# GpSimd adds the two halves of each head's exponentials before VectorE sums them

## The chip, the core and the metric

One core of a Trainium2 chip runs the whole program. TensorE (PE in the rows, its weight loads PEld), VectorE (DVE), ScalarE (ACT), GpSimd (POOL) and SyncE (SP, which here only starts transfers) each work through an instruction list of their own, in order, and meet at semaphores. The metric is the device time of one execution in microseconds (us).

## The reference

A perceiver block on x of 4 x 256 tokens with 256 features: cross attention to 4096 context rows, then local attention, then a mixture of experts. Each stage is added to x. What matters here is the local attention: 16 heads of 16 features, windows of 64 queries that see 128 keys (their own window and the one before), cut by a mask, and a softmax over the keys.

```
scores = jnp.einsum('bnqhd,bnkhd->bnhqk', Qb, Kw) / math.sqrt(dh)
scores = jnp.where(mask[None, :, None, :, :], scores, -jnp.inf)
wts = jax.nn.softmax(scores, axis=-1)
out = jnp.einsum('bnhqk,bnkhd->bnqhd', wts, Vw).reshape(B, N, D)
return out @ o_w.T + o_b
```

## The kernel before, in words

The program has three parts in time. Until about 258 us: cross attention, bound by TensorE. From there to about 338 us: local attention. Then the routing of tokens to experts, and from about 358 us to the end 23 tiles of expert products, in which TensorE works without a pause and the expert weights stream in.

Local attention is cut into 16 units (`WORK`): for each of 4 batch entries, 2 tiles of 128 tokens (t) times 2 halves of the heads (8 heads each, `HPC`). One unit holds 128 queries x 8 heads x 128 keys, so 128 x 1024 numbers; it lies in `local[u]`, of which there are four, part of `region_a`. Unit n goes through these steps:

- TensorE: `local_score(n)`, masks and scores into four PSUM banks (lines 1355, 1360, 1365). There is only one set of these banks, so the scores of unit n wait until VectorE has read those of unit n-1 (`less_max`).
- VectorE: `local_max(n)`, the maximum per head (L963) and the subtraction into `local[u]` (L968, signals `less_max`).
- ScalarE: `local_softmax(n)`, the exponential in place (L788, signals `local_exp`).
- VectorE: `local_sum(n)`, the sum of 128 columns per head (L974) and its reciprocal (L976, signals `inv_ready`).
- GpSimd: the product with the reciprocal, in place (L594, signals `normed`).
- TensorE: `local_turn(n)`, eight transposes (L1290) into two PSUM banks; ScalarE copies them out (`local_evict`, L677); TensorE `local_weigh(n)` multiplies with the values (L1502); ScalarE copies the result out (`local_out`, L801).

The order on each engine is written out by hand. TensorE runs turn(n), score(n+3), weigh(n-1), and then, beside ten of the units, one projection of queries, keys or values of a later batch entry (`FILL_AT`, L1346). VectorE runs sum(n+1), max(n+3). ScalarE runs the copies of unit n, the output of n-1, the exponential of n+3, the projection's copy. GpSimd has only the products, and between them three small jobs: four small operations after unit 2 (`root_second`, L529 to L539), one after unit 3 (L599), and the addition of a bias row to 128 x 512 numbers after unit 5 (`rows_biased`, L546).

`silu0` and `silu1` are parts of `region_w`; they are written only in the expert stage, and nothing lives there during local attention.

Of the kernel before, what the change touches and what calls it, by code (L numbers as in the profile page):

```python
# [8 lines left out]
ALU = mybir.AluOpType  # L9
ACT = mybir.ActivationFunctionType  # L10
X_AXIS = mybir.AxisListType.X

P = 128
# [8 lines left out]
BANK = 512  # L22
# [5 lines left out]
HEADS, DH, WIN = 16, 16, 64  # L28
HPC = P // DH
# [7 lines left out]
WORK = [(b, u) for b in range(BATCH) for u in range(len(UNITS))]  # L37
# [45 lines left out]
def perceiver(nc, x, ctx, ctx_cols, first_weights, w2_b, second_weights, third_weights, o_b, up_weights, down_weights, out):  # L83
    stack = ExitStack()
    with stack:
        def sb(name, cols, dt=F32):
            return stack.enter_context(nc.sbuf_tensor(name, [P, cols], dt))

        def sem(name):
            return stack.enter_context(nc.semaphore(name))  # L90
# [10 lines left out]
        def cut(region, widths):  # L101
            at, parts = 0, []
            for w in widths:
                parts.append(region[:, at:at + w])
                at += w
            assert at <= region.shape[1], (at, region.shape)
            return parts
# [9 lines left out]
        k_side = k_side_f.rearrange("p (a c n) -> p a c n", a=SIDES, c=DC)  # L117
        local = [s.rearrange("p (h k) -> p h k", h=HPC) for s in (sl0, sl1, sl2, sl3)]
        _, pT_f, _, headsT_f = cut(region_s, [TILES * D, 4 * BANK, DC * TOK, DC * TOK])
        pT = pT_f.rearrange("p (r k n) -> p r k n", r=4, k=TPG)  # L120
        v_wide = v_wide_f.rearrange("p (t h n) -> p t h n", t=BATCH * STRIPS, h=HEADS)
# [3 lines left out]
        w_up = [region_a[:, at * MAT:(at + 2) * MAT] for at in (0, 2, 6)]  # L125
        w_down = [region_a[:, (4 + n) * MAT:(5 + n) * MAT] for n in range(2)]
        x3n_f, place_row_f, place_prob_f, _, xrT_f, place_tile_f, _ = cut(
            region_s, [TILES * D, PICKS * P // 2, PARTS * PICKS * EVEN // 2, PICKS * P // 2 - PARTS * PICKS * EVEN // 2,
                       DC * TOK, PARTS * PICKS * EVEN // 2, DC * TOK - PARTS * PICKS * EVEN // 2])
# [2 lines left out]
        xrT = xrT_f.rearrange("p (c n) -> p c n", c=DC)  # L132
        hid = [xrT_f[:, n * INNER:(n + 1) * INNER] for n in range(2)]
        *xg, hidT0, hidT1, yt0, yt1, silu0, silu1 = cut(region_w, [D] * AHEAD + [INNER] * 2 + [D] * 2 + [INNER] * 2)
        hidT, yt, silu = [hidT0, hidT1], [yt0, yt1], [silu0, silu1]
        _, last_tokens, same = cut(region_w, [RAW * DC * BANK - 2 * P, P, P])
        before_last = sb("tokens_before_last", 1)

# [7 lines left out]
        def two_parts(name, cols):  # L146
# [50 lines left out]
        hmax, hsum, hinv = [sb(name, len(UNITS) * HPC)[:, :].rearrange("p (u h) -> p u h", u=len(UNITS))  # L197
                            for name in ("head_max", "head_sum", "head_inv")]
# [58 lines left out]
        zeroed = sem("zeroed")  # L257
        masks_ready, sides_ready = sem("masks_ready"), sem("sides_ready")
        local_done, row_max, less_max, local_exp = sem("local_done"), sem("row_max"), sem("less_max"), sem("local_exp")
        row_sum, inv_ready, normed = sem("row_sum"), sem("inv_ready"), sem("normed")  # L260
        local_turned, localT_ready, localpv_done = sem("local_turned"), sem("localT_ready"), sem("localpv_done")
        heads_ready = sem("heads_ready")
# [75 lines left out]
        def over_keys(cols):  # L338
            return cols.rearrange("p (h a) -> p h a", a=1).broadcast_to([P, HPC, P])
# [117 lines left out]
        def _(pool):  # L457
# [76 lines left out]
            def root_second(b):  # L534
                two = slice(2 * b, 2 * b + 2)
                root(b, SECOND_AT[b], ROOT_SECOND[b])
                nc.gpsimd.tensor_tensor(shift[:, two], mv[:, two, 0], rstd[:, two], ALU.mult).then_inc(shifting, 1)
                pool.wait_ge(shifting, b + 1)
                nc.gpsimd.tensor_tensor(shift[:, two], zeros[:, 0:2], shift[:, two], ALU.subtract).then_inc(bias2_ready, 1)  # L539

            def rows_biased(b):
                part = xr[:, b * TPB:(b + 1) * TPB, :]
                if b == 0:
                    pool.wait_ge(ob_loaded, 16)
                pool.wait_ge(xn_ready, SECOND_AT[b] * TPB)
                nc.gpsimd.tensor_tensor(part, part, obr[:, :].rearrange("p (a d) -> p a d", a=1).broadcast_to([P, TPB, D]),  # L546
                                        ALU.add).then_inc(biased, 1)
# [9 lines left out]
            for b in range(BATCH):  # L557
                n = b % 2
# [30 lines left out]
            nc.gpsimd.memset(v_wide_f[:, KEPT:], 0.0).then_inc(zeroed, 1)  # L589


            for n, (b, u) in enumerate(WORK):
                pool.wait_ge(inv_ready, n + 1)
                nc.gpsimd.tensor_tensor(local[u], local[u], over_keys(hinv[:, u, :]), ALU.mult).then_inc(normed, 1)  # L594
                if n == LAST_ROOT:
                    root_second(BATCH - 1)
                if n == GATE_CENTRED:
                    pool.wait_ge(heads_ready, GATE_MEAN + 1)
                    nc.gpsimd.tensor_tensor(gate, gwT, gate_mean[:, :].rearrange("p (a e) -> p a e", a=1).broadcast_to([P, DC, E]),  # L599
                                            ALU.subtract).then_inc(gate_centred, 1)  # L600
                if n == LAST_BIAS:
                    rows_biased(BATCH - 1)
# [294 lines left out]
        def _(dve):  # L897
# [72 lines left out]

            def local_sum(n):
                b, u = WORK[n]
                dve.wait_ge(local_exp, n + 1)
                nc.vector.tensor_reduce(hsum[:, u, :], local[u], axis=X_AXIS, op=ALU.add).then_inc(row_sum, 1)  # L974
                dve.wait_ge(row_sum, n + 1)
                nc.vector.reciprocal(hinv[:, u, :], hsum[:, u, :]).then_inc(inv_ready, 1)  # L976

# [128 lines left out]

            local_max(1)
            local_sum(0)
            local_max(2)
            for n in range(len(WORK)):  # L1110
                if n + 1 < len(WORK):
                    local_sum(n + 1)
                if n + LOOK < len(WORK):
                    local_max(n + LOOK)
                if n == 0:
                    statistics(range(TILES - TPB, TILES))
# [115 lines left out]
            def tile_y(j, n):  # L1232
# [7 lines left out]
                else:  # L1240
# [7 lines left out]
                                    axis=X_AXIS, op=ALU.add).then_inc(tokens_ready, 1)  # L1248
            for j in range(SLOT_TILES):
                n = j % 2  # L1250
# [485 lines left out]
```

## Time and profile before

| | |
|---|---|
| median of 3 runs | 600.28 us (600.08 to 600.31) |
| the profiled execution's own time | 599.96 us |
| its span, first to last instruction | 598.2 us |
| granted TensorE clock, mean | 0.989 |
| PE busy | 571.6 us, 96% |
| DVE busy | 414.6 us, 69% |
| ACT busy | 332.5 us, 56% |
| POOL busy | 254.5 us, 43% |

Busy is time in which an engine has an instruction in work; for TensorE the ends are modelled, so a busy PE need not be at its peak. The share is a mean over stages that have different limits. In the rows, "[1.04 <-POOL region_a L594]" means that the engine stood idle for 1.04 us before this instruction and that the signal which ended the idle time came from GpSimd's line 594. PEclk 1.00 is the full clock of 2.4 GHz, 0.50 is 1.2 GHz.

### The profile page before, as it was taken

Reading aid. Unit: us, or ns where it says so; the run is one execution under the profiler, and the core shown is the slowest. Engines: PE = TensorE matmul, PEld = TensorE weight load, DVE = VectorE, ACT = ScalarE, POOL = GpSimd, SP = SyncE. Lnnn points to the kernel's source line nnn. Section 1 sums busy time; section 2 is a strip of 40 time slices with the busy share of each in tenths; the row PEclk is TensorE's granted clock in tenths of the full one; section 3 lists DMA queues with packets and bytes.
Section 4 is the critical chain, followed back from the end, with each engine's and each line's share of the span. In section 5 each row is a group of like instructions: output and inputs, shape, how many; then the busy total and the mean of one; then the engine's idle time right before and its main releaser. Section 6 shows DMA issues by size and latency. Waiting matters only on the chain.

```text
span 598.2 us, 9977 instructions
## 1 busy us (share of the span) xinstructions
PE 571.6 (96%) x3765; PEld 487.6 (82%) x3765; DVE 414.6 (69%) x701; ACT 332.5 (56%) x564; POOL 254.5 (43%) x259
## 2 busy tenths in 40 slices
PE   7799999999999999989999989999999999999995
PEld 5589988998799889967676867888888888888884
DVE  3866686668656865579888688676767676777761
ACT  4337535753476455628766827565647474747450
POOL 6366347534742484334544620333333333333212
PEclk9999999999999999999999989999999999999998
DMA  8993086008600200000002966999999999999642
GB/s 291 424 413 157 1 329 233 1 2 324 239 1 2 71 1 2 1 1 1 2 2 75 397 260 240 339 323 342 332 345 329 339 333 354 337 343 323 226 154 88
DMA packets 25166, 119.27 MB, mean 199 GB/s; under 512 B 2640, under 2 KB 8912, under 8 KB 14096
## 3 DMA queue, kind: packets, MB, share of 16 engines
q1 hardware_dynamic: 20752, 112.48, 49.9%
q0 software_dynamic: 4368, 6.16, 5.3%
q8 instruction: 30, 0.49, 0.3%
q14 instruction: 16, 0.13, 0.1%
HBM read 113.52 MB, written 6.42 MB: 200 GB/s over the span
## 4 chain that ended last, share of the span: by engine, by line
PE 80%; DVE 11%; ACT 2%; issue 2%; POOL 2%; DMA 2%; POOLq 0%; SPq 0%; DVEq 0%; ACTq 0%
PE psum L1653 20%; PE psum L1430 14%; PE psum L1670 13%; PE psum L1384 12%; PE psum L1290 11%; PE psum L1346 2%; DVE head_max L963 2%; DVE region_a L968 1%; DMA region_w<-ctx_cols_dram 1%; PE psum L1528 1%; POOL wide_low L562 1%; DVE wide_low L985 1%; PE psum L1312 1%; PE psum L1392 1%; PE psum L1502 1%
## 5 line engine op out<-in xcount | busy, mean ns | idle before, releaser
L677 ACT ACTIVATE wide_high<-region_a 128x1024 fp32r<-128x1024 f32 (+1 forms) x104 | 105.2, 1011 | 97.7 <-PE psum L1653 90.2
L1120 DVE TENSOR_TENSOR wide_low<-region_a,wide_high 128x1024 fp32r<-128x1024 f32 x92 | 112.4, 1224 | 58.2 <-ACT wide_high L677 58.2
L1670 PE MATMUL psum<-region_a,region_w 128*128 128x256 f32 x368 | 83.3, 379 | 0.0
L1430 PE MATMUL psum<-turned_high,wide_low 128*128 128x256 f32 x256 | 78.6, 307 | 2.9 <-DVE turned_low L1046 2.4
L1046 DVE TENSOR_TENSOR turned_low<-psum,turned_high 128x512 fp32r<-128x512 f32 x64 | 43.7, 690 | 54.2 <-ACT turned_high L677 54.1
L1653 PE MATMUL psum<-wide_low,turned_high 128*128 128x512 f32 x184 | 78.2, 425 | 0.2 <-DVE turned_high L1222 0.2
L1670 PEld LDWEIGHTS psum<-region_a,region_w 128*128 128x128 f32 x368 | 69.7, 190 | 10.0
L1653 PE MATMUL psum<-wide_high,turned_low 128*128 128x512 f32 x184 | 72.5, 394 | 0.0
L1430 PE MATMUL psum<-turned_high,wide_high 128*128 128x256 f32 x256 | 72.2, 282 | 0.0
L1430 PE MATMUL psum<-turned_low,wide_high 128*128 128x256 f32 x256 | 72.1, 282 | 0.0
L1653 PE MATMUL psum<-wide_high,turned_high 128*128 128x512 f32 x184 | 72.1, 392 | 0.0
L1290 PE MATMUL psum<-ident,region_s 128*128 128x128 f32 x448 | 63.0, 273 | 0.9 <-DVE region_s L923 0.4
L629 POOL TENSOR_TENSOR pool_pause<-zeros 128x1 f32<-128x1 f32 x21 | 4.0, 191 | 139.1 <-DVE region_w L1239 139.1
L677 ACT ACTIVATE turned_high<-psum 128x512 fp32r<-128x512 f32 x64 | 37.9, 599 | 40.8 <-PE psum L1430 40.2
L562 POOL TENSOR_TENSOR wide_low<-region_w,wide_high 128x1024 fp32r<-128x1024 f32 x12 | 31.9, 2657 | 66.2 <-ACT wide_high L677 66.2
L1030 DVE TENSOR_SCALAR_CACHE_REDUCE region_s<-psum 128x512 f32<-128x512 f32 x64 | 43.2, 687 | 22.1 <-PE psum L1384 22.1
L722 ACT ACTIVATE region_s<-region_s,neg_max 128x512 f32<-128x512 f32 x64 | 45.9, 718 | 19.9 <-DVE neg_max L1034 19.9
L1384 PE MATMUL psum<-wide_high,wide_low 128*128 128x512 f32 x128 | 51.7, 404 | 5.4 <-DVE wide_low L985 4.3
L1290 PEld LDWEIGHTS psum<-ident,region_s 128*128 128x128 f32 x448 | 51.6, 140 | 6.0 <-ACT region_s L722 2.0
L576 POOL CAST wide_high<-region_a 128x512 fp32r<-128x512 f32 x52 | 36.5, 710 | 44.7 <-PE psum L1430 35.5
L677 ACT ACTIVATE wide_high<-region_w 128x1024 fp32r<-128x1024 f32 x32 | 33.6, 1059 | 38.7 <-PE psum L1384 28.9
L1430 PEld LDWEIGHTS psum<-turned_high,wide_low 128*128 128x128 f32 x256 | 48.5, 189 | 4.3 <-POOL wide_low L579 2.5
(223 smaller groups left out, 1196.3 us busy)
## 6 DMA issues: line engine op xcount, KB each, us to landing
region_a<-up_weights_dram SPq DMA_DIRECT2D x23, 2048.0 KB, 9.1
region_a<-down_weights_dram SPq DMA_DIRECT2D x23, 1024.0 KB, 7.3
region_w<-ctx_cols_dram SPq DMA_DIRECT2D x32, 512.0 KB, 9.3
region_a<-ctx_dram SPq DMA_DIRECT2D x16, 1024.0 KB, 12.2
third_weights<-third_weights_dram SPq DMA_DIRECT2D x1, 1035.0 KB, 26.0
residual<-x_dram SPq DMA_DIRECT2D x4, 256.0 KB, 7.8
sums_by_token<-residual SPq DMA_DIRECT2D x2, 512.0 KB, 9.5
normed_rows<-region_s SPq DMA_DIRECT2D x4, 256.0 KB, 6.6
```

The source lines that it names most:

```text
L562: nc.gpsimd.tensor_tensor(ctxT_lo[:, split_of(b, ch)], raw[(b * CHUNKS + ch) % RAW], ctxT_hi[:, split_of(b, ch)].bitcast(F32), ALU.subtrac ...
L576: nc.gpsimd.tensor_copy(val_hi[:, at], part).then_inc(val_high, 1)
L677: return nc.scalar.activation(dst, src, ACT.Copy)
L722: nc.scalar.activation(part, part, ACT.Exp, bias=nmax[:, t:t + 1], accum_out=lpart[:, t, k:k + 1]).then_inc(exp_done, 1)
L1030: nc.vector.tensor_scalar(scores[t][:, ch * BANK:(ch + 1) * BANK], score_bank(ch, t), float(D) ** -0.5, LOWEST, ALU.mult, ALU.max, accum_o ...
L1046: nc.vector.tensor_tensor(pT_lo[:, g % 2], probs_bank(g).rearrange("p (k n) -> p k n", k=PAIR), pT_hi[:, g % 2].bitcast(F32), ALU.subtract ...
L1120: nc.vector.tensor_tensor(w_lo[:, k % RING], group_of(k), w_hi[:, k % RING].bitcast(F32), ALU.subtract).then_inc(low_ready, 1)
L1290: return nc.tensor.transpose(dst, src, ident[0:src.shape[0], 0:src.shape[0]])
L1384: last = nc.tensor.matmul(score_bank(ch, t), q[:, n, c, t * P:(t + 1) * P], k[:, split_of(b, ch), c, :], start=c == 0 and m == 0, stop=c = ...
L1430: last = nc.tensor.matmul(bank[6 + c][:, 0:NTOK], v[:, value_slot(b, g), k, c * P:(c + 1) * P], p[:, g % 2, k, :], start=g == 0 and k == 0 ...
L1653: last = nc.tensor.matmul(bank[g], rows[:, n, cols], w[:, (4 * j + g) % RING, c, :], start=c == 0 and m == 0, stop=c == DC - 1 and m == le ...
L1670: last = nc.tensor.matmul(to[:, 0:D], hidT[n][:, ic * P:(ic + 1) * P], rows, start=ic == 0, stop=ic == IC - 1)
```

## The change

Before the sum, GpSimd adds columns 64 to 127 of each head to columns 0 to 63, into one of two areas of 128 x 512 in `silu0`; VectorE then sums 64 columns per head in place of 128. The sum no longer waits for the exponential but for the new addition (`halved`), which waits for the exponential. The exponentials themselves stay as they are for the product. GpSimd's list becomes: add 0, add 1, product 0, add 2, product 1, add 3, and so on.

```diff
+        halves = [h.rearrange("p (h k) -> p h k", h=HPC) for h in (silu0[:, 0:BANK], silu0[:, BANK:])]
...
+            def add_halves(n):
+                u = WORK[n][1]
+                pool.wait_ge(local_exp, n + 1)
+                nc.gpsimd.tensor_tensor(halves[n % 2], local[u][:, :, 0:WIN], local[u][:, :, WIN:P], ALU.add).then_inc(halved, 1)
+
+            add_halves(0)
+            add_halves(1)
             for n, (b, u) in enumerate(WORK):
                 pool.wait_ge(inv_ready, n + 1)
                 nc.gpsimd.tensor_tensor(local[u], local[u], over_keys(hinv[:, u, :]), ALU.mult).then_inc(normed, 1)
+                if n + 2 < len(WORK):
+                    add_halves(n + 2)
                 if n == LAST_ROOT:
                     root_second(BATCH - 1)
...
             def local_sum(n):
                 b, u = WORK[n]
-                dve.wait_ge(local_exp, n + 1)
-                nc.vector.tensor_reduce(hsum[:, u, :], local[u], axis=X_AXIS, op=ALU.add).then_inc(row_sum, 1)
+                dve.wait_ge(halved, n + 1)
+                nc.vector.tensor_reduce(hsum[:, u, :], halves[n % 2], axis=X_AXIS, op=ALU.add).then_inc(row_sum, 1)
```

GpSimd's list at the start of local attention, before. L594 is the product; the four rows behind it are `root_second`.

```order
L594 TENSOR_TENSOR region_a<-region_a,head_inv 128x1024 [waits inv_ready] x3
L529 TENSOR_TENSOR ln_sd<-ln_mean_var,eps 128x2 [waits var_ready]
L531 TENSOR_TENSOR ln_rstd<-ln_sd,minus_half 128x2 [waits sd_ready]
L537 TENSOR_TENSOR ln_shift<-ln_mean_var,ln_rstd 128x2 [waits rstd_ready]
L539 TENSOR_TENSOR ln_shift<-zeros,ln_shift 128x2 [waits shifting]
```

The same place on GpSimd now. L597 is the new addition, L603 the product, L531 to L541 are `root_second`.

```order
L597 TENSOR_TENSOR region_w<-region_a 128x512 [waits local_exp] x2
L603 TENSOR_TENSOR region_a<-region_a,head_inv 128x1024 [waits inv_ready]
L597 TENSOR_TENSOR region_w<-region_a 128x512 [waits local_exp]
L603 TENSOR_TENSOR region_a<-region_a,head_inv 128x1024 [waits inv_ready]
L597 TENSOR_TENSOR region_w<-region_a 128x512 [waits local_exp]
L603 TENSOR_TENSOR region_a<-region_a,head_inv 128x1024 [waits inv_ready]
L597 TENSOR_TENSOR region_w<-region_a 128x512 [waits local_exp]
L531 TENSOR_TENSOR ln_sd<-ln_mean_var,eps 128x2 [waits var_ready]
L533 TENSOR_TENSOR ln_rstd<-ln_sd,minus_half 128x2 [waits sd_ready]
L539 TENSOR_TENSOR ln_shift<-ln_mean_var,ln_rstd 128x2 [waits rstd_ready]
L541 TENSOR_TENSOR ln_shift<-zeros,ln_shift 128x2 [waits shifting]
```

Every product but the last two now stands behind the addition of a later unit, which waits for that unit's exponential. The order on the other engines is the same.

## Rows read from the trace of the kernel before

**Rows 1.** Stretches: busy us and instructions of PE, PEld, DVE, ACT, POOL; PEclk, DMA, GB/s.
```profile
258.00:332.00 74.00, 68.65 (x801) 50.08 (x800) 65.45 (x80) 47.72 (x93) 36.61 (x23) 1.00 0.09 33
345.00:598.20 253.20, 244.34 (x1248) 205.79 (x1247) 174.72 (x255) 137.13 (x185) 79.15 (x70) 0.99 0.85 294
```
**Rows 2.** Waits, 260 to 332 us: us in total, times, longest.
```profile
POOL region_a L594 <- DVE head_inv L976: 36.2, 15, 5.1
...
DVE head_max L963 <- PE psum L1365: 4.0, 5, 1.3
...
PE psum L1290 <- POOL region_a L594: 1.6, 3, 1.0
```
**Rows 3.** Timeline, 321 to 327 us, units 11 to 15: start, duration, engine, line.
```profile
321.49 1.23 DVE L968 TENSOR_TENSOR region_a<-psum,head_max 128x1024 f32<-128x1024 f32 x1
...
322.40 1.04 PE L1290 MATMUL psum<-ident,region_a 128*128 128x128 f32 x8
322.63 1.21 DVE L974 TENSOR_REDUCE head_sum<-region_a 128x8 f32<-128x1024 f32 x1
322.75 1.06 ACT L788 ACTIVATE region_a<-region_a 128x1024 f32<-128x1024 f32 x1 [1.32 <-DVE region_a L968]
...
323.27 0.60 PE L1355 MATMUL psum<-mask_bf,ident_bf 128*128 128x256 bf16 x4
...
323.88 0.20 DVE L976 RECIPROCAL head_inv<-head_sum 128x8 f32<-128x8 f32 x1
324.16 1.90 POOL L594 TENSOR_TENSOR region_a<-region_a,head_inv 128x1024 f32<-128x1024 f32 x1 [2.05 <-DVE head_inv L976]
...
324.60 1.23 DVE L963 TENSOR_REDUCE head_max<-psum 128x8 f32<-128x1024 f32 x1 [0.52 <-PE psum L1365]
...
325.93 1.23 DVE L968 TENSOR_TENSOR region_a<-psum,head_max 128x1024 f32<-128x1024 f32 x1
...
326.11 1.09 PE L1290 MATMUL psum<-ident,region_a 128*128 128x128 f32 x8 [1.04 <-POOL region_a L594]
```
**Rows 4.** Durations by line: ns least, median, most; first and last start.
```profile
L594 POOL TENSOR_TENSOR region_a<-region_a,head_inv x16: 1895/1897/1898, 267.0 to 330.4; 128x1024 f32<-128x1024 f32 x16
...
L546 POOL TENSOR_TENSOR residual<-residual,ob_rows x4: 1280/1284/1288, 94.5 to 291.3; 128x512 f32<-128x512 f32 x4
...
L579 POOL TENSOR_TENSOR wide_low<-region_a,wide_high x32: 1272/1292/2262, 35.7 to 245.3; 128x512 fp32r<-128x512 f32 x32
```
**Rows 5.** VectorE's groups by form: busy us and mean ns of one.
```profile
L1090 DVE TENSOR_TENSOR residual<-residual,psum 128x512 f32<-128x512 f32 x3 | 2.0, 664 | 0.0
```
**Rows 6.** Timeline, the first units, all engines.
```profile
266.02 1.05 ACT L788 ACTIVATE region_a<-region_a 128x1024 f32<-128x1024 f32 x1
...
267.04 1.90 POOL L594 TENSOR_TENSOR region_a<-region_a,head_inv 128x1024 f32<-128x1024 f32 x1 [5.05 <-DVE head_inv L976]
...
268.99 1.10 PE L1290 MATMUL psum<-ident,region_a 128*128 128x128 f32 x8 [0.18 <-POOL region_a L594]
...
272.50 1.22 DVE L968 TENSOR_TENSOR region_a<-psum,head_max 128x1024 f32<-128x1024 f32 x1
```
**Rows 7.** Timeline of GpSimd: the two jobs between the products.
```profile
277.94 0.20 POOL L529 TENSOR_TENSOR ln_sd<-ln_mean_var,eps 128x2 f32<-128x2 f32 x1
...
279.27 0.20 POOL L539 TENSOR_TENSOR ln_shift<-zeros,ln_shift 128x2 f32<-128x2 f32 x1
...
291.34 1.28 POOL L546 TENSOR_TENSOR residual<-residual,ob_rows 128x512 f32<-128x512 f32 x1
```
**Rows 8.** Timeline of TensorE, one unit with a full projection.
```profile
295.95 1.04 PE L1290 MATMUL psum<-ident,region_a 128*128 128x128 f32 x8
...
298.57 1.99 PE L1346 MATMUL psum<-xnT,third_weights 128*128 128x256 f32 x8
300.40 1.04 PE L1290 MATMUL psum<-ident,region_a 128*128 128x128 f32 x8
```
**Rows 9.** Two short stretches, columns as in rows 1.
```profile
260.00:264.00 4.00, 3.00 (x20) 1.85 (x19) 3.93 (x7) 1.06 (x1) 1.98 (x1) 1.00 0.00 0
344.00:348.00 4.00, 3.70 (x24) 2.22 (x25) 2.96 (x14) 1.72 (x5) 0.20 (x1) 0.50 1.08 395
```

More of the change, by code:

```diff
@@ L259, in perceiver @@
         local_done, row_max, less_max, local_exp = sem("local_done"), sem("row_max"), sem("less_max"), sem("local_exp")
+        halved = sem("halved")
         row_sum, inv_ready, normed = sem("row_sum"), sem("inv_ready"), sem("normed")
```

## The prediction, made before the result was known

> **What bounds the kernel now.** I read the stretches first, since the change touches local attention alone. There TensorE is busy 68.65 of 74 us and VectorE 65.45; GpSimd has the most room, 36.61 of 74 [rows 1]. The waits say who is late. GpSimd waits 36.2 us in total for VectorE's reciprocal; VectorE waits for scores, 4.0 us for one form of them; TensorE waits only 1.6 us, three times, for GpSimd's product [rows 2]. So no single engine sets the pace. A unit with a full projection costs TensorE 300.40 - 295.95 = 4.45 us back to back [rows 8]; where there is less beside it, a loop through the engines decides.
>
> That loop is read in the timeline of units 11 to 15 [rows 3]. Call S(n) the start of the subtraction L968 of unit n. From S(14) at 321.49: the sum of unit 13 starts 1.14 us later (322.63), its reciprocal 1.25 later (323.88), the product 0.28 later (324.16), the transposes of unit 13 1.95 later (326.11, TensorE idle 1.04 before them). The steps behind are read one unit earlier: transposes 322.40, scores 323.27 (0.87), maximum 324.60 (1.33), subtraction 325.93 (1.33). The scores behind turn(13) are those of unit 16, which does not exist; for lower units they are those of n+3. So S(n+2) leads by sum(n+1), product(n+1), turn(n+1), score(n+4) to S(n+4): 1.14 + 1.25 + 0.28 + 1.95 + 0.87 + 1.33 + 1.33 = 8.15 us for two units. There are two such loops, one of even units and one of odd. TensorE's 4.45 per full unit (8.90 for two) is the longer of the two limits in most of the stage; over the stage the kernel takes S(15) - S(3) = 325.93 - 272.50 = 53.43 us for 12 units [rows 3, 6], 8.9 for two.
>
> **The change, part by part.**
>
> *VectorE's sum* goes from 1.21 us [rows 3] to 512 inputs. A 512 form takes 664 ns where the 1024 form of L968 takes 1225 [rows 3, 5], so 512 fewer cost 0.56 less: about 0.65, and 16 x 0.56 = 9 us less VectorE busy time. It is hidden or worse, as the next part shows.
>
> *GpSimd's addition* is new: 16 x 128x512 with two real operands. The nearest row is L546, an addition with the same count of outputs: 1284 ns, once in this very stage beside VectorE's sum [rows 4, 7]. I take 1.28, so 20.5 us more GpSimd busy time. The low end is half of the product's 1897, 0.95; the high end is the slowest L579, 2.26 [rows 4]. Below zero is excluded, it is added work.
>
> The Trainium skill ("GPSIMD Engine Reference", section "3.1 Elementwise — side-by-side cycle accounting") puts a two-input addition at some 2.6 cycles of 1.2 GHz per element. For 512 that would be an estimate of 1.11 us, which makes the sum below 4.6 in place of 5.6; the trace has 1.28 for this count, and that is used.
>
> *The new wait* is where the time goes. GpSimd works in order, and product(n+1) now stands behind add(n+2), which waits for the exponential of unit n+2. From S(n+2): the exponential starts 322.75 - 321.49 = 1.26 later and takes 1.06; with 0.07 to reach GpSimd and 1.23 from start to start for the addition (its 1.28 less the overlap seen between neighbours), product(n+1) can start 3.63 us after S(n+2). Before it started 1.14 + 1.25 + 0.28 = 2.67 after. The shorter sum does not help: sum(n+1) needs only add(n+1), done a unit earlier, and the reciprocal is ready about 1.14 + 0.70 + 0.28 = 2.12 after S(n+2), but the product is not next in the list. So the loop becomes 8.15 + 0.96, about 9.13 us for two units (4.56 per unit), above TensorE's 4.45. Queued behind the late product are turn(n+1), and on TensorE behind that score(n+4), weigh(n), and the projection; VectorE's max(n+4) waits for that score.
>
> *The sum over the stage*, on the odd loop, which reaches the last unit:
> - Start. Product 0 stands behind add 1, which waits for exp(1), done at 266.02 + 1.05 = 267.07. Add 1 ends at 268.40, product 0 starts there and not at 267.04: +1.35, about 1.3 of which turn(0), at 268.99, score(3) and S(3) take over [rows 6]. S(3) = 273.8.
> - Six rounds from S(3) to S(15): 6 x 9.13 = 54.8.
> - In one of them the bias job after unit 5 (1.28, 1.25 net) stands between add(7) and product 6; before it lay in idle time [rows 7]. +1.25. The four small operations after unit 2 (277.94 to 279.47, 1.5 us) now delay product 3 in the same way. That falls on the even loop; the two loops share TensorE, and a turn, a score or a projection of the one standing ahead of the other's costs 0.1 to 0.5 us at four places. I put all of this at 1.4.
> - S(15) = 273.8 + 54.8 + 1.25 + 1.4 = 331.25 against 325.93: +5.3.
> - Behind it TensorE runs without a pause, and its backlog (13 late product, output rows, two last units) adds 0.2 to 0.3. Local attention ends 5.6 later.
>
> Routing is a chain of dependent steps and the expert stage has TensorE busy 244.34 of 253.20 us [rows 1]; nothing there gives time back. The weights' first load starts when the last scores are done, so it moves with them. Profile: 599.96 + 5.6 = 605.6; on the median of the runs (0.32 above the profiled execution) 605.9.
>
> **The rivals.**
>
> *It is faster.* Place: the product after the reciprocal. If the additions fitted into GpSimd's 36.2 us of waiting [rows 2] and never stood ahead of a ready product, each of some five bound rounds would gain up to the sum's 0.56, 2.8 us in all: 597.5. It decides at the point where add(n+2) is over when the reciprocal n+1 arrives: 2.12 after S(n+2). The exponential alone ends 2.32 after, so even a free addition does not get there. Chance 3%.
>
> *No change.* TensorE, at 93% busy, would hide the late products: turn(6) is at 295.95 with no idle time before it [rows 8]. The slack before a turn is 1.5 us at most, and it is used up in the first units because 9.13 is above 8.90. 600.3. Chance 3%.
>
> *The addition is cheaper* (0.95). The loop becomes 8.80, the start +1.0; TensorE decides more often: +3.8, 604.1. Chance 14%.
>
> *The addition is stretched* by VectorE beside it, to the 2.26 seen once for L579. Seven times 0.98 more on the loop, and TensorE no cover any more, bring about 12 us: 612. Against it: the product kept 1895 to 1898 ns in all 16 cases beside VectorE's maxima, subtractions and sums [rows 4]. Chance 4%.
> The Trainium skill ("SBUF — State Buffer", section "Who interferes with whom") says that a VectorE instruction with two SBUF inputs and a GpSimd one that reads SBUF exclude each other. In this stage VectorE's large operations have one SBUF or PSUM tensor, so by that rule too the addition keeps its time, and the 16 rows agree.
>
> *The clock falls.* TensorE will idle some 6 us more. The clock stayed at 1.00 with 3.00 of 4 us busy, and was 0.50 at 344 to 348, behind the small products of the routing [rows 9]. A fall in the stage for 4 to 8 us would cost half of that on TensorE's work: 2 to 4 more, 608 to 610. A shift of the low spell in routing is worth up to 1 us either way. Chance 6%.
>
> **How the numbers follow.** The forecast holds 70%, with its own range 604.6 to 607.2 (addition 1.1 to 1.4, TensorE places 0.5 to 2.4). The range reaches to the cheap addition and to part of the clock case: 603.4 to 608.3. What a measurement of this kernel can tell from no change is 0.2%, 1.2 us. Slower: 70 + 14 + 4 + 6 = 94, less 1 for what I may have overlooked, 93%; same 3.5%; faster 3.5%.
>
> **What the profile after would show.** L597 16 times at about 1280 ns; the sum (L985) at about 650 ns. GpSimd busy near 275 us and VectorE near 406. Product 0 starts near 268.4, not 267.0; in late units it starts 3.6 us after the subtraction of the next unit, directly behind an addition, and GpSimd waits for ScalarE's exponential. TensorE waits for the product in more than three places, some 7 us in all. S(15) lies near 331.3, and from there all steps lie 5.3 to 5.8 later. I am wrong if the product starts within 2.7 us of that subtraction, if GpSimd's products are not behind additions, if the addition is far from 1.28, or if the delay of local attention is not the same as that of the end.

## The result and the profile after

| | before | after |
|---|---|---|
| median of 4 runs | 600.18 us (598.35 to 600.31) | 606.12 us (604.40 to 611.34) |
| ratio | | 1.0134, 95% interval 1.0106 to 1.0162 |
| profiled execution, its span | 599.96, 598.2 us | 604.40, 602.6 us |
| GpSimd busy | 254.5 us | 274.6 us |
| VectorE busy | 414.6 us | 405.9 us |

The kernel is slower. The forecast was 605.9 us in a range of 603.4 to 608.3. A second comparison, of 6 runs with 23 of before, gave 1.0081 (1.0053 to 1.0110), so the loss is between 3 and 10 us, 4.6 and 5.9 by the two medians. Both intervals lie clear of no change.

The waits from 260 to 337 us, where [rows 2] has those of before:

```profile
POOL region_w L597 <- ACT region_a L799: 24.8, 15, 3.1
...
DVE head_max L974 <- PE psum L1376: 11.4, 8, 2.8
...
DVE head_max L974 <- PE psum L1371: 8.3, 6, 3.4
PE psum L1301 <- POOL region_a L603: 7.0, 9, 1.5
```

L597 is the addition, L603 the product, L985 the sum. GpSimd no longer waits for the reciprocal at all. It waits for the exponential, 15 times, and what TensorE waits for the product grew from 1.6 us in 3 places to 7.0 in 9. VectorE's saved time came back as waiting for scores: 19.7 us now, 6.2 before (4.0 behind L1365 and 2.2 behind L1360, the lines that are L1376 and L1371 here). Durations by line (ns least, median, most):

```profile
L597 POOL TENSOR_TENSOR region_w<-region_a x16: 1266/1270/1275, 261.8 to 333.7; 128x512 f32<-128x512 f32 x16
...
L603 POOL TENSOR_TENSOR region_a<-region_a,head_inv x16: 1892/1897/1901, 267.4 to 336.8; 128x1024 f32<-128x1024 f32 x16
...
L985 DVE TENSOR_REDUCE head_sum<-region_w x16: 654/676/687, 264.6 to 335.0; 128x8 f32<-128x512 f32 x16
```

The loop, in the timeline from 326 to 332 us. These are units 12 to 15 as in [rows 3]:

```profile
326.40 1.23 DVE L979 TENSOR_TENSOR region_a<-psum,head_max 128x1024 f32<-128x1024 f32 x1
327.54 0.68 DVE L985 TENSOR_REDUCE head_sum<-region_w 128x8 f32<-128x512 f32 x1
327.66 1.06 ACT L799 ACTIVATE region_a<-region_a 128x1024 f32<-128x1024 f32 x1 [1.63 <-DVE region_a L979]
...
328.25 0.20 DVE L987 RECIPROCAL head_inv<-head_sum 128x8 f32<-128x8 f32 x1
...
328.79 1.27 POOL L597 TENSOR_TENSOR region_w<-region_a 128x512 f32<-128x512 f32 x1 [1.12 <-ACT region_a L799]
...
330.02 1.90 POOL L603 TENSOR_TENSOR region_a<-region_a,head_inv 128x1024 f32<-128x1024 f32 x1
...
331.31 1.23 DVE L979 TENSOR_TENSOR region_a<-psum,head_max 128x1024 f32<-128x1024 f32 x1
...
331.97 0.33 PE L1301 MATMUL psum<-ident,region_a 128*128 128x128 f32 x1 [1.52 <-POOL region_a L603]
```

The reciprocal of unit 13 is out at 328.45, and GpSimd is idle until 328.79. It does not start product 13, because addition 14 is next in its list and that waits for the exponential. The product starts at 330.02, 3.62 us after the subtraction at 326.40 (3.63 was forecast, 2.67 before). It shows no idle time of its own: an engine that is never idle before an instruction can still have made it late, by what it was told to do first.

A second thing is in this profile that is not in the one of before. Stretches from 293 us on, columns as in [rows 1]:

```profile
293.00:294.00 1.00, 0.20 (x1) 0.20 (x2) 0.99 (x2) 0.65 (x2) 0.74 (x1) 0.87 0.00 0
294.00:295.00 1.00, 1.00 (x6) 1.00 (x6) 0.20 (x1) 1.00 (x3) 0.44 (x1) 0.50 0.00 0
...
296.00:297.00 1.00, 1.00 (x7) 0.59 (x9) 0.00 (x0) 0.40 (x1) 1.00 (x1) 0.50 0.00 0
297.00:298.00 1.00, 1.00 (x24) 0.45 (x20) 0.38 (x1) 0.00 (x0) 1.00 (x2) 0.92 0.00 0
```

TensorE ran at 1.2 GHz for some 3.4 us, behind two waits that the timeline of TensorE shows:

```profile
291.99 0.63 PE L1301 MATMUL psum<-ident,cross_outT 128*128 128x128 f32 x4 [0.67 <-ACT cross_outT L710]
293.80 1.97 PE L1301 MATMUL psum<-ident,region_a 128*128 128x128 f32 x8 [1.18 <-POOL region_a L603]
```

The eight transposes took 1.97 us instead of 1.09.

From here on "stage length" is the distance from the subtraction of unit 0 to that of unit 15. It is read from one profile and leaves out what the clock does before and behind the stage. Before: 325.93 - 260.40 = 65.53. After: 331.31 - 259.45 = 71.86, so +6.33.

### The profile page after: what moved, and what is told of

Same layout as the page of the kernel before. It is cut to its first block, busy times and chain, and to the rows that moved or that the text cites. A ratio compares the mean times of both kernels' runs of the same rounds, so it can differ in the third digit from the quotient of the medians.

```text
span 602.6 us, 9993 instructions
## 1 busy us (share of the span) xinstructions
PE 574.7 (95%) x3765; PEld 488.9 (81%) x3765; DVE 405.9 (67%) x701; ACT 332.5 (55%) x564; POOL 274.6 (46%) x275
## 4 chain that ended last, share of the span: by engine, by line
PE 78%; DVE 9%; POOL 5%; issue 3%; DMA 2%; ACT 2%; POOLq 0%; DVEq 0%; ACTq 0%
PE psum L1664 19%; PE psum L1441 14%; PE psum L1395 12%; PE psum L1681 12%; PE psum L1301 11%; PE psum L1357 2%; POOL region_a L603 2%; DVE head_max L974 1%; POOL region_w L597 1%; DVE region_a L979 1%; PE psum L1323 1%; ACT region_a L799 1%; POOL wide_low L564 1%; PE psum L1539 1%; PE psum L1403 1%
```

## The experiments

| kernel | stage length | median us | ratio to before, 95% |
|---|---|---|---|
| before | 65.53 | 599.13 and 599.86 | 1 |
| changed, again (e1) | 71.84 | 603.72 | 1.0081 (1.0053 to 1.0110) |
| product first (e2) | 64.35 | 599.61 | 1.0013 (0.9996 to 1.0029) |
| additions, full sum (e3) | 71.85 | 602.61 | 1.0066 (1.0044 to 1.0088) |
| short sum, no additions (e4) | 64.73 | 598.77 | 0.9990 (0.9976 to 1.0004) |
| filled waits (e5) | 71.42 | 605.27 | 1.0087 (1.0056 to 1.0118) |
| bias job first (e6) | 70.28 | 603.81 | 1.0084 (1.0054 to 1.0114) |
| half additions (e7) | 68.29 | 602.30 | 1.0047 (1.0025 to 1.0068) |
| product first, plain tail (e8) | 64.36 | 598.37 | 0.9974 (0.9956 to 0.9993) |

e1 to e4 were measured beside one set of 23 runs of the kernel before (median 599.13), e5 to e8 beside a second of 29 (599.86).

**The changed kernel again (e1).** No edit.

> The changed kernel once more, unaltered, to see how much of its distance is the same in every execution. Stage length here and below means: start of unit 0's subtraction to start of unit 15's, 65.53 us before and 71.86 in the first profile of the changed kernel, of which I put 0.9 to 1.0 down to 3.4 us at half the TensorE clock inside the stage. Theory (product behind the addition in GpSimd's list): 70.9 without such a clock spell, 71.9 with it, end +5 to +6 us. Rival (the clock spell is the larger part of the loss and comes and goes): without it the end is within 3 us of the kernel before.

71.84, and half clock again, from about 294.7 to 298.1 us. Its six runs went from 602.19 to 606.94 us. The three with a mean clock of 0.990 to 0.993 took 602.2 to 602.6, the three at 0.984 to 0.987 took 604.8 to 606.9. The runs of before took 597.3 to 599.6 us at 0.990 to 0.994 and 599.6 to 600.8 at 0.984 to 0.987. By the medians of these groups the loss is some 4 us at the higher clock and some 5 at the lower. The rival of 3 us or less without the half clock falls too, by an estimate from the mean clock. In each of the twelve profiles the mean is 1 less the lost share, where a spell of 3.4 us at half clock counts as 1.7 us lost. All twelve lose 3.4 us in the routing, and a half clock in the stage loses 1.7 more, 5.1 together. A run at 0.993 can have lost at most 4.5 (0.0075 of its span). So the two runs at 0.993 had none in the stage, and they took 602.2 and 602.6 us, some 5 more than the run of before at 0.994 (597.3).

**Product first (e2).**

```diff
             add_halves(0)
-            add_halves(1)
...
-                if n + 2 < len(WORK):
-                    add_halves(n + 2)
+                if n + 1 < len(WORK):
+                    add_halves(n + 1)
```

> GpSimd's list becomes add 0, product 0, add 1, product 1, add 2 and so on: the same 16 additions, but no product stands behind the addition of a later unit. Theory (order in GpSimd's list): stage length 64.3 us, 1.1 shorter than before, because the shorter sum now counts; at the end the last addition, sum and product stand in one row, so the last product is late and the end of the kernel comes 0 to 1.5 us later than before, 5 earlier than the changed kernel. Rival (the additions themselves cost, by stretching VectorE or GpSimd or by filling GpSimd): stage length stays above 70 and the end at +5.

64.35 against the 64.3 expected. GpSimd does the same 16 additions of 1272 ns, and the whole loss of the stage is gone. At the end it is 0.5 us behind the kernel before by the medians (0 to 1.5 expected) and 4.1 ahead of e1. From its timeline, GpSimd and VectorE:

```profile
320.09 1.23 DVE L978 TENSOR_TENSOR region_a<-psum,head_max 128x1024 f32<-128x1024 f32 x1
...
321.43 0.69 DVE L984 TENSOR_REDUCE head_sum<-region_w 128x8 f32<-128x512 f32 x1
322.15 0.20 DVE L986 RECIPROCAL head_inv<-head_sum 128x8 f32<-128x8 f32 x1
322.44 1.90 POOL L602 TENSOR_TENSOR region_a<-region_a,head_inv 128x1024 f32<-128x1024 f32 x1 [1.04 <-DVE head_inv L986]
...
324.29 1.27 POOL L597 TENSOR_TENSOR region_w<-region_a 128x512 f32<-128x512 f32 x1
```

The product is 2.35 us behind the subtraction, the addition follows it. This sets the price of the order against the price of the work.

**Additions where they are, full sum from the exponentials (e3).** The product gets a wait for its own unit's addition, since the sum no longer stands for it. That addition is further up in the same list.

```diff
                 pool.wait_ge(inv_ready, n + 1)
+                pool.wait_ge(halved, n + 1)
...
-                dve.wait_ge(halved, n + 1)
-                nc.vector.tensor_reduce(hsum[:, u, :], halves[n % 2], axis=X_AXIS, op=ALU.add).then_inc(row_sum, 1)
+                dve.wait_ge(local_exp, n + 1)
+                nc.vector.tensor_reduce(hsum[:, u, :], local[u], axis=X_AXIS, op=ALU.add).then_inc(row_sum, 1)
```

> The additions stay where the change put them, but VectorE sums 128 columns from the exponentials as before and does not wait for them. Theory: the loss is whole, stage length 71.0 (71.9 with a clock spell), end +5.7, since the product waits in GpSimd's own list and not through the sum. Rival (the loss comes from VectorE waiting for the addition): stage length near 65.5, end near 0.

71.85: the loss does not need VectorE to wait for anything new, and the shorter sum gives nothing back. In GpSimd's and VectorE's rows the reciprocal still comes before the addition is over:

```profile
329.35 0.20 DVE L988 RECIPROCAL head_inv<-head_sum 128x8 f32<-128x8 f32 x1
329.35 1.27 POOL L597 TENSOR_TENSOR region_w<-region_a 128x512 f32<-128x512 f32 x1 [1.10 <-ACT region_a L800]
...
330.58 1.89 POOL L604 TENSOR_TENSOR region_a<-region_a,head_inv 128x1024 f32<-128x1024 f32 x1
```

Its end, +3.5 us by the medians, is less than the +5.7 expected; by the profile alone it is +5.3 (605.24 against 599.96). Four of its six runs, at 0.990 to 0.993, took 601.9 to 602.7 us, the other two, at 0.985, 605.2 and 605.5.

**Short sum, no additions (e4).** `halves` is filled once with ones, and the sum reads it after the exponential.

> No additions; VectorE sums 64 columns of a constant area, so the weights are not normalised by their own sums: this leaves out half of the softmax sum. It prices the saving by itself. Theory: VectorE's 0.53 us per unit is worth 1.1 us of stage length (64.3) and 1.1 us at the end, the rest is hidden by TensorE. Rival (VectorE bounds the stage, its saving is worth most of 16 x 0.53): stage length under 60, end -5 or more.

64.73, 0.8 shorter than before, not the 6 and more of the rival. Up to S(14) it is 59.92, as in e2 and 1.17 shorter than before (61.09); only S(15) then comes 0.4 later than in e2, behind a wait of VectorE of 0.47 us for TensorE's transposes, which I did not follow. At the end no difference can be told (0.9976 to 1.0004), nor is the 1.1 us expected there excluded. VectorE's 16 x 0.53 = 8.5 us are hidden, all but about 1 of stage length.

**Idle matmuls in the two waits (e5).**

```diff
+                    warm(2)
                     rows_turn(BATCH - 1)
...
+                if n == LAST_BIAS:
+                    pe.wait_ge(heads_ready, n - 1)
+                    for _ in range(4):
+                        nc.tensor.matmul(bank[6][:, 0:D], zeros[:, 0:P], zeros[:, 0:D], start=True, stop=True)
                 pe.wait_ge(normed, n + 1)
```

> The changed kernel, with six idle matmuls on zeros put into TensorE's two waits around unit 5 (two before the transposes of the normed rows, four before those of unit 5), which nothing waits for. In both profiles of the changed kernel the clock fell to half for 3.4 us right behind these waits. If the fall follows from them: no fall between 288 and 300 us, stage length 70.9 to 71.1 in place of 71.85, and 0.5 to 1.5 us less at the end than the changed kernel. If it has another cause: the fall stays, length 71.8 or more.

No half clock in the stage, but I mis-sized the filling:

```profile
291.69 1.13 PE L1306 MATMUL psum<-zeros 128*128 128x256 f32 x4
...
293.57 1.99 PE L1556 MATMUL psum<-zeros 128*128 128x256 f32 x8 [0.32 <-ACT region_s L812]
295.40 1.04 PE L1301 MATMUL psum<-ident,region_a 128*128 128x128 f32 x8
```

Four such matmuls are eight rows and take 1.83 us to the next instruction, where 1.2 had been idle, so the transposes of unit 5 came at 295.40 instead of 294.18 (e1). The length fell only by 0.4, and the end did not improve. From the routing's first maximum to the end this profile is also 1.5 us longer than that of e1 (255.8 against 254.3). I did not find out why.

**Bias job first (e6).**

```diff
+                if n == LAST_BIAS:
+                    rows_biased(BATCH - 1)
                 if n + 2 < len(WORK):
                     add_halves(n + 2)
...
-                if n == LAST_BIAS:
-                    rows_biased(BATCH - 1)
```

> The changed kernel with the bias job after unit 5 put ahead of addition 7 in GpSimd's list, where 0.82 us of its 1.25 fall into waiting time. My term of 1.25 says: product 6 starts 0.8 to 0.9 us earlier and the stage is 0.8 shorter, 71.0 to 71.1 with the clock spell, 70.1 without. If GpSimd's small jobs are hidden anyway, the length stays at 71.85.

70.28, and the clock stayed at 1.00 in the whole stage. So two things differ, and 71.86 - 70.28 = 1.58 is what they cost together. GpSimd's rows show the job in what had been waiting time:

```profile
294.35 1.28 POOL L548 TENSOR_TENSOR residual<-residual,ob_rows 128x512 f32<-128x512 f32 x1
295.58 1.28 POOL L597 TENSOR_TENSOR region_w<-region_a 128x512 f32<-128x512 f32 x1
296.81 1.90 POOL L603 TENSOR_TENSOR region_a<-region_a,head_inv 128x1024 f32<-128x1024 f32 x1
```

Counted from S(0), product 6 starts 0.86 us earlier (36.71 against 37.57), as expected. But the rows of the changed kernel, VectorE and then TensorE, show that it was not what the stage waited for there:

```profile
297.62 1.23 DVE L974 TENSOR_REDUCE head_max<-psum 128x8 f32<-128x1024 f32 x1 [3.40 <-PE psum L1371]
298.95 1.23 DVE L979 TENSOR_TENSOR region_a<-psum,head_max 128x1024 f32<-128x1024 f32 x1
...
298.05 1.99 PE L1357 MATMUL psum<-xnT,third_weights 128*128 128x256 f32 x8
299.88 1.04 PE L1301 MATMUL psum<-ident,region_a 128*128 128x128 f32 x8
```

And in e6:

```profile
296.68 1.23 DVE L974 TENSOR_REDUCE head_max<-psum 128x8 f32<-128x1024 f32 x1 [1.82 <-PE psum L1371]
298.01 1.23 DVE L979 TENSOR_TENSOR region_a<-psum,head_max 128x1024 f32<-128x1024 f32 x1
```

S(8), counted from S(0), is 39.50 in the changed kernel and 37.91 in e6. The whole 1.59 is there already, and this subtraction needs the transposes of unit 5 and the scores behind them, which ran at half clock, but not product 6. Product 6 was over at 298.92, and turn(6) started only at 299.88, directly behind a projection, so beside the half clock the job cost next to nothing. At full clock TensorE would have come to turn(6) sooner and waited for product 6, until about 0.9 before 299.88. By that estimate the half clock costs 0.9 with the job in its old place, and the job the other 0.7. No run has the job in its old place and a full clock, so this split is read from rows and not measured.

The gain does not show in the ratio (1.0084 against 1.0081 of e1), whose intervals are 3 to 4 us wide.

**Half additions (e7).** As e3, with `WIN // 2` columns per operand.

> As the kernel with additions and a full sum from the exponentials, but each addition covers 32 columns of a head in place of 64, 256 numbers per partition, so it takes about 0.69 us in place of 1.27; its result isn't used by anything. Theory: the loop falls from 9.13 to 8.5 us for two units, below TensorE's 8.9, and TensorE decides: stage length 68.0 to 68.2, end +2.4 to +2.6 against the kernel before. Rival (loss in proportion to the addition's time): half of the loss, length 68.7, end +2.9.

The addition took 726 ns, not 690, and the length is 68.29: 0.1 above the forecast, 0.4 below the rival's. Against e3, 0.55 us less per addition brought 3.56, some 0.9 of it (e6) the half clock, which did not appear. Without that, 2.8 of 5.4 us are left with 57% of the addition's time; in proportion to the time it would be 3.1, 68.6. Single rounds of two units tell the two readings apart better. The last, S(13) to S(15), takes 8.39 before, 9.17 in e3 and 8.61 here, which is 9.17 less the 0.55 of the shorter addition; in proportion it would be 8.83. The round S(9) to S(11) takes 9.62 before, 9.61 in e3 and 9.61 here: in it the addition does not count at all. Both fit the loop with a floor set elsewhere, and not a loss in proportion. It is one profile of this kernel.

**Product first, plain tail (e8).** As e2, but units 14 and 15 are summed as before the change, without an addition.

> Product first, as in the kernel that was as fast as the one before, and units 14 and 15 summed by VectorE over 128 columns without an addition, so that the last products don't wait for additions. Theory: stage length 64.3 and the end 1.1 us earlier than before, 0.7 to 1.8 earlier than the product-first kernel. Rival (the end is set by something else in the last units or by the clock's spells): within 0.5 us of the kernel before.

0.9974 (0.9956 to 0.9993): 1.5 us faster than the kernel before. The stage is as long as in e2. (Against e2 it is 1.2 us by the medians and 2.3 by the ratios, each taken beside its own runs of before; 0.7 to 1.8 was expected.) What differs is the end of GpSimd's list. In e2 the last two products stand apart, with addition 15 between them:

```profile
326.66 1.90 POOL L602 TENSOR_TENSOR region_a<-region_a,head_inv 128x1024 f32<-128x1024 f32 x1 [1.10 <-DVE head_inv L986]
328.51 1.27 POOL L597 TENSOR_TENSOR region_w<-region_a 128x512 f32<-128x512 f32 x1
330.82 1.90 POOL L602 TENSOR_TENSOR region_a<-region_a,head_inv 128x1024 f32<-128x1024 f32 x1 [1.04 <-DVE head_inv L986]
```

In e8 they stand together, and counted from S(0) the last is over 1.8 us earlier (330.60 - 259.82 = 70.78 against 332.72 - 260.17 = 72.55):

```profile
326.85 3.75 POOL L603 TENSOR_TENSOR region_a<-region_a,head_inv 128x1024 f32<-128x1024 f32 x2 [2.86 <-DVE head_inv L991]
```

From S(15) to the routing's first maximum it takes 18.31 us before, 19.43 in e2 and 18.27 in e8. So e2 lost behind the stage what it had gained in it, and e8 does not.

**Two more profiles.**

> A third profile of the changed kernel, to see whether the fall of the clock behind the waits around unit 5 belongs to it. If it does: half clock for 3.4 us between 292 and 298 us, stage length 71.85, end 604 to 607. If it comes and goes: no fall, stage length 70.9, end 602 to 603.

71.82, half clock again, from about 295.5 to 298.9; 606.42 us, where a run of before beside it took 600.22. That makes 4 of 4 profiles with the bias job behind addition 7 and additions of 1.27 us (the changed kernel three times, and e3).

> A second profile of the kernel with the bias job ahead of addition 7. TensorE's two waits around unit 5 are as long there as in the changed kernel, yet its first profile had no fall of the clock. If the fall depends on when the wait comes and not on its length alone, this profile may show one: stage length 71.1 with it, 70.3 without.

70.27, no half clock in the stage; 601.74 us. So 0 of 2 here, though TensorE's waits at that place are the same 0.67 and 1.18 us. The fall does not follow from the length of those two waits alone. It did not come and go within one kernel's profiles, but by the mean clocks of e1 it is not in every execution of the changed kernel either, so 4 of 4 against 0 of 2 does not show that the order in GpSimd's list decides it. For the same reason the one profile of e5 without it does not show that filling the waits prevents it.

## Why the prediction was right, point by point

**Mechanism.** Right, and shown: putting the product first (e2) removes the loss with all additions kept, and keeping the additions in their place without the new wait of the sum (e3) keeps it whole.

**Start.** Forecast +1.3 at S(3). Measured from S(0): 272.88 - 259.45 = 13.43 against 272.50 - 260.40 = 12.10, +1.33.

**Loop.** 9.13 us for two units was forecast. S(11), S(13), S(15) are at 313.00, 322.15 and 331.31: 9.15 and 9.16. The step from before is smaller than the 0.96 forecast: the last rounds of before took 8.40 and 8.39, not the 8.15 that I had added up, so there the loop grew by about 0.8.

**Bias job.** Forecast +1.25 in one round, which is that of S(7) to S(9). For product 6 this holds: moving the job brings it forward by 0.86 (e6), and the other 0.39 then still lies before it (it starts 4.01 after S(7), its neighbours 3.62). For the stage I had taken it as additive, and it is not. Of the 0.86, some 0.7 would count at full clock and next to nothing counts beside the half clock.

**TensorE's places.** 1.4 was put down for four places. S(3) to S(15) took 331.31 - 272.88 = 58.43; less 54.8 and 1.25 that leaves 2.4. The half clock accounts for about 0.9 of it by the estimate in e6, so 1.5 is left. The six rounds took 9.17, 10.12, 11.22, 9.61, 9.15 and 9.16, so the extra time lies in the second to the fourth. In e6, without the half clock, S(3) to S(15) took 56.85, 2.05 more than 54.8, some 0.4 of it the rest of the bias job. The size of 1.4 holds roughly, though the places were not measured one by one.

**The clock.** A rival of 6% that half came true: the fall did come, in every profile of the changed kernel, for 3.4 us, and cost about 0.9 beside the bias job (an estimate, e6) and not the 2 to 4 I gave. I had argued from the one quiet stretch of [rows 9] that it would stay up.

**Behind the stage.** I had the sign wrong. I added 0.2 to 0.3 for a backlog of TensorE. Measured from S(15) to the routing's first maximum (L1160, before L1149), it was 348.61 - 331.31 = 17.30 against 344.24 - 325.93 = 18.31, so 1.0 us less. The last 24 small products of the gate (L1584) took 2.78 us instead of 3.42 at L1573, since the low spell of the routing, at 342 to 350 us before, came at 348 to 356, behind them. The other 0.4 lies before them. TensorE waited there 0.53 us for ScalarE's copy at an output product (L1528) before, and not at all now (L1539).

**The sum.** +6.33 in the stage, -1.01 behind it, and the profile's stage began 0.95 earlier than that of before, for no reason in the change (the low spell of the first 32 us lay elsewhere): 4.4 in the spans, 602.6 - 598.2. On the median it was +5.9, where 5.6 was forecast; the second comparison (e1) gave +4.6, so the runs do not say on which side of 5.6 the loss lies. Two errors of about 1 us, the half clock in the stage and the 1.0 behind it, cancelled. The agreement to 0.2 us is luck. Less the half clock the stage grew by about 5.4, where 5.3 was forecast, and there the start and the late rounds are right by their own rows. The profile's own time, 604.40, is 1.2 below the 605.6 that I gave it.

**The addition.** 1.28 taken, 1270 ns measured, with no stretch in 16. The Trainium skill's 2.6 cycles per element for a two-input addition ("GPSIMD Engine Reference", section "3.1 Elementwise — side-by-side cycle accounting") made an estimate of 1.11. By e7's row, 256 elements fewer save 1270 - 726 = 544 ns, 2.1 ns or 2.55 cycles of 1.2 GHz per element, so slope and page agree; what the estimate lacked is the fixed part, some 180 ns.

**Rivals.** Neither the cheaper nor the stretched addition came (1266 to 1275 ns), and TensorE did not hide the late products: it waited 7.0 us for them. "It is faster" was tied to the point at which an addition is over when the reciprocal comes. That is right for this order only. I had not asked what another order would give, and with the product first the same additions leave the stage 1.2 us shorter than before (e2), and with the plain tail the kernel is faster (e8).

## What to carry to other kernels

When work is moved to an idle engine, its busy share says little; read what stands behind the new instruction in that engine's list, and what the new instruction waits for. Put the product that others wait for first and the preparatory work behind it, in the slack that its result has (in e2 the sum of unit 14 starts 5.58 us after its subtraction, 320.09 to 325.67, room for the exponential, a product and the addition). At the ends of such a pipeline, where there is no next unit to hide it, leave the old form in place.

## What the runs showed that was not expected

TensorE's clock went to 1.2 GHz for 3.4 us in the middle of a stage in which it is busy nearly 90% of the time (69.69 of 79.5 us), behind waits of 0.67 and 1.18 us within 2 us. It did so in 4 of 4 profiles of two kernels and in 0 of 2 of a kernel in which TensorE waits just as long at the same places. By the mean clock, two of the six runs in e1 cannot have had it. What decides it stays open.

Executions of one kernel differ by some 4 to 5 us, in the first runs of the changed kernel by 6.9 and in e6 by 8.5, in large part with the mean clock: 29 runs of the kernel before took 597.1 to 598.2 us at 0.994 and 600.8 to 601.7 at 0.982 to 0.986. That is as much as the effect studied here, so the stage length in a profile, which repeated within 0.04 us (71.86, 71.84, 71.82), was the sharper measure.
